# Cross attention with a quantised feed-forward on one core: a reordered prologue, another queue for the second weights, and moved steps in every stage

## What is computed

```python
# attention: 32 query heads of 16, 8 key/value groups, 256 keys from ctx
q = ln(x) @ Wq.T + bq;  k = ctx @ Wk.T + bk;  v = ctx @ Wv.T + bv
scores = einsum("bgrqd,bgkd->bgrqk", q, k) / 4, masked with -inf (two masks)
x = x + softmax(scores) @ v  (heads joined)  @ Wo.T + bo
# feed-forward: both products with quantised rows and weights
bitlinear(x, w, b) = einsum("bsd,od->bso", act_quant(rms_norm(x)), weight_quant(w)) + b
h = gelu(silu(bitlinear(ln(x), w1, b1)))            # 2048 wide
out = x + bitlinear(layer_norm(h) * g + b, w2, b2)
```

## Time and profile before

| | us |
|---|---|
| three runs | 619.96, 621.9, 622.6 (median 621.9) |
| the profiled execution, own time | 622.59 |
| its span, first to last instruction | 620.8 |
| PE busy | 524.9 (85%) |
| DVE busy | 489.0 (79%) |
| ACT busy | 350.8 (57%) |
| POOL busy | 135.0 (22%) |
| mean granted clock of TensorE | 0.926 of full speed |
| the ends of the stages c = 0, 1, 2, 3, 4, 5, 6 on PE | about 109, 182, 248, 310, 373, 435, 498 |

### The profile page before, as it was taken

One profiled execution on the slowest core, in us unless ns is written; L12 is line 12 of the kernel. 1 busy time (PEld: TensorE's weight loads), 2 busy tenths in 40 slices (PEclk: granted clock), 3 DMA queues, 4 the chain that ended last, 5 costly groups with the idle time before them and its releaser, 6 DMA issues.

```text
span 620.8 us, 8914 instructions
## 1 busy us (share of the span) xinstructions
PE 524.9 (85%) x3374; PEld 289.5 (47%) x3374; DVE 489.0 (79%) x728; ACT 350.8 (57%) x424; POOL 135.0 (22%) x101
## 2 busy tenths in 40 slices
PE   4778497689889999999999999999869969698446
PEld 4666133362456355645564556455425523343222
DVE  3769939349699978997899789988896887648784
ACT  0244280517584867486748674867187739287630
POOL 5030031100611061106110611301140113103220
PEclk9989598797989999999999999999969989799688
DMA  8588637934422641365136412642134221100000
GB/s 315 152 234 324 211 84 191 386 116 146 86 67 105 183 99 36 125 195 114 36 124 191 102 54 76 191 98 74 40 86 102 74 75 17 38 0 1 34 34 35
DMA packets 32994, 72.17 MB, mean 116 GB/s; under 512 B 7167, under 2 KB 14529, under 8 KB 29950
## 3 DMA queue, kind: packets, MB, share of 16 engines
q1 hardware_dynamic: 31798, 71.26, 38.8%
q10 hardware_dynamic: 1152, 0.31, 0.2%
HBM read 46.50 MB, written 20.61 MB: 108 GB/s over the span
## 4 chain that ended last, share of the span: by engine, by line
PE 58%; DVE 12%; DMA 10%; ACT 9%; issue 7%; SPq 2%; POOL 1%; ACTq 1%; DVEq 0%
PE FF L853 9%; PE FF L678 7%; PE PV L792 7%; PE FF L901 6%; ACT PT L1069 5%; PE PV L775 5%; PE S L759 5%; PE S L735 5%; DVE negm L1337 4%; PE S L888 3%; PE FF L855 2%; PE PV L735 2%; DMA work<-in_w 2%; PE FF L867 2%; DMA num<-o_raw 2%
## 5 line engine op out<-in xcount | busy, mean ns | idle before, releaser
L1069 ACT ACTIVATE PT<-S 128x1024 f32<-128x1024 f32 x128 | 123.6, 1033 | 28.1 <-PE S L759 28.0
L1337 DVE TENSOR_REDUCE negm<-S 128x4 f32<-128x1024 f32 x88 | 105.6, 1215 | 24.7 <-PE S L735 23.2
L759 PE MATMUL S<-Q,K 100*128 100x512 bf16 x256 | 78.0, 413 | 27.7 <-ACT PT L1069 18.3
L775 PE MATMUL PV<-PT,vaug 128*32 128x256 f32 x1024 | 71.8, 400 | 0.4 <-ACT PT L1069 0.4
L853 PE MATMUL FF<-w1t,xqT 128*128 128x512 bf16 x256 | 67.4, 386 | 2.0 <-ACT PT L1100 1.1
L1100 ACT ACTIVATE work<-FF,s 128x512 f32<-128x512 f32 x56 | 38.5, 687 | 40.6 <-PE FF L855 40.6
L792 PE MATMUL PV<-wo_sb,num 128*128 128x512 f32 x128 | 59.9, 614 | 0.4 <-DVE negm L1337 0.4
L678 PE MATMUL FF<-xnT,wq_sb 128*128 128x256 f32 x224 | 52.8, 394 | 8.6 <-ACT xnT L1039 8.6
L735 PE MATMUL S<-K,Q 97*128 97x256 bf16 x352 | 54.5, 282 | 6.6 <-issue 3.5
L759 PEld LDWEIGHTS S<-Q,K 100*128 100x128 bf16 x256 | 18.7, 101 | 77.4 <-ACT PT L1069 54.8
L1337 DVE TENSOR_REDUCE negm<-PV 128x4 f32<-128x1024 f32 x40 | 48.8, 1221 | 6.3 <-PE PV L735 5.9
(11 more groups left out here) (196 smaller groups left out, 858.5 us busy)
## 6 DMA issues: line engine op xcount, KB each, us to landing
Q<-q_d SPq DMA_DIRECT2D x15, 768.0 KB
work<-in_w SPq DMA_DIRECT2D x8, 1024.0 KB, 11.4
q_d<-part SPq DMA_DIRECT2D x8, 768.0 KB, 3.6
x_sb<-in_x SPq DMA_DIRECT2D x8, 512.0 KB, 4.0
ctx_sb<-in_ctxT SPq DMA_DIRECT2D x8, 512.0 KB, 4.0
q_d<-part SPq DMA_DIRECT2D x8, 512.0 KB, 3.3
xb_sb<-in_x SPq DMA_DIRECT2D x8, 512.0 KB, 3.9
rec<-rec_d SPq DMA_DIRECT2D x30, 128.0 KB, 2.6
```

Of the source, the lines that this page charges most:

```text
L759: last = pe.matmul(where, K[0:ROWS_2, g, kt * P:(kt + 1) * P], Q[0:ROWS_2, g, 2 * pair:2 * pair + 2, :], start=not masked, stop=True)
L775: last = pe.matmul(PV[32 * r:32 * r + 32, g % 4, :], vaug[:, c % 2, kt, g, :], PT[:, n % PT_SLOTS, r, :], start=(kt == 0), stop=(kt == TT ...
L1069: act.activation(PT[:, n % PT_SLOTS, :, :], ST[n % 2][:], ACT.Exp, scale=0.25).then_inc(S["pt_made"], 1)
L1337: dve.tensor_reduce(negm[:, t, R * g:R * g + R], RING_1[n % 3][:], AX.X, ALU.max, negate=True).then_inc(S["max_made"], 1)
```

## The change

In the order of the code:

- Q parts: `q_d` has four blocks of 16 rows instead of six. Part 0 is written once (block 0), part 1 twice (blocks 1 and 3), part 2 once. `query_rows` reads block 0 three times over into Q's rows 0 to 47 in one transfer and the other three blocks in a second one; `ROW_LOADS` is 4.
- Prologue: bk has a semaphore of its own. PE does K, `turn_x(0)`, V, `project_q(0)`; ACT and DVE follow suit (`keys`, `values_in`; `key_rests(0)` ahead of `masks`; `maximum(0, 0)` ahead of `key_rests(1)`). SP issues x(1) before ctx(1), one chunk of w1 behind the key parts, and x(2) and the other three chunks behind `rows_back_first`.
- w2: POOL issues the four chunks at the head of stage c = 0, as soon as `w1_done` is set; its weight sum, scale and quantising move up in stage c = 1. `rows_back(a, 1)` is issued ahead of the last denominators and numerators.
- Stage heads on PE: `project_out(f, 0)`, `turn_max`, the weight sum, `turn_x(w)`, `project_out(f, 1)`, `project_q(w)`, `project_k(a)`; `project_v(a)` stands behind the first pair of `scores_2`, and its copy on ACT behind the second exp.
- ACT: where there is no w, `squares(t, 1)` stands behind the second exp; in stage c = 7 both squares stand between the exps. The means are made by ACT behind each gelu, not by POOL.
- Last stages: `turn_hq` of batch 5 goes to four halves of S1 and S0 (`turned_hq_ps`), so that `layer_1` needn't wait for it; steps on DVE and PE are reordered.

```diff
-Q_TERMS = [slice(0, 3), slice(3, 6, 2), slice(4, 5)]
+Q_BLOCKS = [slice(0, 1), slice(1, 4, 2), slice(2, 3)]
+        def turned_hq_ps(t, n):
+            where = S0w if t == B - 3 and n > 1 else S1w
+            return where[:, 512 * (n % 2):512 * (n % 2) + 512]
...
@@ SP
-            weight_chunk(w1, 0)
-            weight_chunk(w1, 1)
+            def query_rows(a, gs, landed):
+                shared = q_d[a][0:HD, gs, :].rearrange("d g n -> d (g n)")
+                sp.dma_start(Q[0:Q_SHARED * HD, gs, :, :].rearrange("d g r t -> d (g r t)"),
+                             shared.unsqueeze(0).broadcast_to([Q_SHARED] + list(shared.shape))).then_inc(landed, 16)
+                sp.dma_start(Q[Q_SHARED * HD:ROWS_SPLIT, gs, :, :].rearrange("d g r t -> d (g r t)"),
+                             q_d[a][HD:4 * HD, gs, :].rearrange("d g n -> d (g n)")).then_inc(landed, 16)
...
                 if at_start(a):
+                    load_x(1)
                     load_context(1)
-                    load_x(1)
                     key_parts(0)
-                    load_x(2)
+                    weight_chunk(w1, 0)
                     query_parts(0)
                     negatives()
                     rows_back_first()
-                    weight_chunk(w1, 2)
-                    weight_chunk(w1, 3)
+                    load_x(2)
+                    for n in range(1, 4):
+                        weight_chunk(w1, n)
...
                     denominators(c, 2)
-                    denominators(c, 3)
-                    numerators(c, 1)
                 if a is not None:
                     rows_back(a, 1)
                 if c is not None:
+                    denominators(c, 3)
+                    numerators(c, 1)
...
@@ POOL
+            def second_weights():
+                pool.wait_ge(S["w1_done"], 1)
+                for n in range(4):
+                    cols = slice(2048 * n, 2048 * n + 2048)
+                    pool.dma_start(work[:, cols], w2[:, cols]).then_inc(S[f"w2_chunk{n}"], 16)
...
+                if at_start(c):
+                    second_weights()
                 if w is not None and w + 1 < B:
                     norm_1(w + 1)
...
-                    mean_3(f, 0)
                     norm_3_last(f, 0)
-                    mean_3(f, 1)
                     norm_3_last(f, 1)
...
@@ PE
                 w = next_front(a) if c != 0 else None
-                if w is not None:
-                    turn_x(w)
                 if f is not None:
                     project_out(f, 0, c)
                 if c is not None:
                     turn_max(c)
+                if at_start(c) or at_start(f):
+                    weight_sum(c)
+                if w is not None:
+                    turn_x(w)
+                if f is not None:
+                    project_out(f, 1, c)
                 if w is not None:
                     project_q(w)
-                if f is not None:
-                    project_out(f, 1, c)
                 if a is not None and a > 1:
-                    project_kv(a)
-                if at_start(c) or at_start(f):
-                    weight_sum(c, a)
+                    project_k(a)
                 for g in range(G + 1):
...
+                    if g == 0 and a is not None and a > 1:
+                        project_v(a)
...
                     for n in range(4):
-                        turn_hq(t, n, f)
+                        turn_hq_last(t, n)
                     for n in range(4):
-                        layer_1(f, n, t)
+                        layer_1(f, n, None)
...
-                    layer_1(f, 0, None)
-                    layer_1(f, 1, None)
+                    for n in range(8):
+                        layer_1(f, n, None)
                     layer_2_last(t - 1, 1)
-                    for n in range(2, 8):
-                        layer_1(f, n, None)
...
@@ ACT
+                act.wait_ge(S["gelu_made"], 2 * f + t + 1)
+                act.activation(st[:, 1, t:t + 1], st[:, 0, t:t + 1], ACT.Identity, scale=-1.0 / INNER
+                               ).then_inc(S["mu_made"], 1)
...
-                    squares(t, 0)
                     act.activation(table_call[:, 1:2], table_call[:, 0:1], ACT.Exp)
                     for n in range(16):
                         exps(c, n)
-                        if n == 3:
-                            squares(t, 1)
+                        if n in (1, 3):
+                            squares(t, n // 2)
...
-                if t is not None and a is not None:
+                if t is not None and w is not None:
                     squares(t, 1)
...
-                    keys_and_values(a)
+                    keys(a)
                 if c is not None:
                     for n in range(16):
                         exps(c, n)
+                        if n == 1 and w is None and t is not None:
+                            squares(t, 1)
+                        if n == 1 and a is not None and a > 1:
+                            values_in(a)
...
@@ DVE, last_scores
                 maximum_2(t, 0)
                 power_2(t)
+                maximum_2(t, 1)
                 turn_1(f)
-                maximum_2(t, 1)
+                reciprocal_last(c)
                 factor_2(t)
                 scale_2(t)
-                reciprocal_last(c)
...
@@ DVE, last_hidden and last_values
+                maximum_2(t, 0)
                 residual_2(t - 1, 1)
-                maximum_2(t, 0)
...
                 gain(t, 0)
+                shift(t, 0)
                 spread_last(t, 1)
-                shift(t, 0)
                 gain(t, 1)
...
@@ DVE, body
                 if c is not None:
                     max_rows(c)
+                if at_start(c) or at_start(f):
+                    weight_scale(c)
...
+                if at_start(f):
+                    quantise_weight(1, w2t[:].rearrange("p k n -> p (k n)"))
                 if w is not None:
                     query_rests(w)
```

More of the change, by code:

```diff
@@ L36 @@
 PT_SLOTS = 4
-ROW_LOADS = 3
+ROW_LOADS = 4
 PIECES = 4
@@ L393, in weights_and_biases, with layer_rows @@
                     sp.dma_start(b1_rows[n:n + 1, :], b1_d[cb:cb + 1, :]).then_inc(S["k_b1r"], 16)
-            def second_weights():
-                sp.wait_ge(S["w1_done"], 1)
-                for n in range(4):
-                    weight_chunk(w2, n)
+            def layer_rows():
                 for to, of in ((b2_bc, b2), (g_bc, ln_g), (b_bc, ln_b)):
@@ L453, in body @@
                 if c is not None:
+                    denominators(c, 3)
+                    numerators(c, 1)
+                if c is not None:
                     reciprocals(c)
                 if at_start(c):
-                    second_weights()
+                    layer_rows()
                 if t is not None:
@@ L698, in project_kv, with project_v @@
                 for k in range(KD):
-                    pe.matmul(to[:, 0:T], wkv_sb[:, k, 0:P], ctx_sb[:, k, :],
-                              start=(k == 0), stop=(k == KD - 1))
+                    last = pe.matmul(to[:, 0:T], wkv_sb[:, k, 0:P], ctx_sb[:, k, :],
+                                     start=(k == 0), stop=(k == KD - 1))
+                last.then_inc(S["k_ps"], 1)
+            def project_v(a):
+                if a == 1:
+                    pe.wait_ge(S["v_placed"], 1)
+                to = pair_of(a)
                 for t in range(TT):
@@ L751, in scores_2 @@
                     pe.wait_ge(S["m_in"], 16 * c + 16)
+                if n == 1 and c == 1:
+                    pe.wait_ge(S["w_mean"], 4)
                 if n >= 2:
@@ L875, in turn_hq_last @@
                 pe.wait_ge(S["hs_made"], 2 * t + tok + 1)
-                pe.wait_ge(S["hqT_made"], 4 * t + n - 1)
+                if t > B - 3:
+                    pe.wait_ge(S["hqT_made"], 4 * t + n - 1)
                 for k in range(8):
-                    last = pe.transpose(S1w[:, 512 * half:512 * half + 512].bitcast(BF16)[:, k * P:(k + 1) * P],
+                    last = pe.transpose(turned_hq_ps(t, n).bitcast(BF16)[:, k * P:(k + 1) * P],
                                         source[:, tok, (8 * half + k) * P:(8 * half + k + 1) * P], identb[:])
@@ L1048, in queries, with keys, values_in @@
                                    ).then_inc(S["q_made"], 1)
-            def keys_and_values(a):
-                act.wait_ge(S["kv_ps"], a + 1)
+            def keys(a):
+                act.wait_ge(S["k_ps"], a + 1)
                 wait_for(act, S["k_out"], 48 * a)
                 if at_start(a):
-                    act.wait_ge(S["w_bias"], 48)
+                    act.wait_ge(S["w_bk"], 16)
                 act.activation(part[:, 0, R, :], pair_of(a)[:, 0:T], ACT.Identity, bias=bk_sb[:, 0:1]
                                ).then_inc(S["k_made"], 1)
+            def values_in(a):
+                act.wait_ge(S["kv_ps"], a + 1)
                 if at_start(a):
@@ L1169, in body @@
                 if at_start(a):
```

(33 more changed lines are left out.)

69 lines of the change are left out of this document (28 added, 41 removed).

## The result

The changed kernel takes 680.05 us (median of 4 runs, 677.7 to 689.2), the kernel before 621.0 in the same comparison: ratio 1.094, 95% interval 1.088 to 1.100. One run of it (689.2 us) and one of the kernel before with the broadcast load (668.3 us) were in a slower state, and all ratios, and the costs in us that are called means, leave these two out. The profiled execution has a span of 676.2 us and a mean granted clock of 0.893 (0.926 before). The forecast was 606.5 us, with 615 as the upper end.

The account below looks back on a forecast made before the run. TensorE was taken to bound the middle stages, with idle time at the edges. From 622.6 us, terms summing to -15.7 and the median's -0.7 gave 606.2, say 606.5 us; range 599 to 615.

Parts of the forecast that it names:

- The step that failed: Row loads of later stages: one broadcast load of three equal Q blocks carries the same bytes, one issue more; no cost.
- Start, +4.3: Prologue to scores_2 of batch 0: row loads leave 4.6 us earlier, but x(2) lands at about 42; loss 4.3 us.
- c = 0, 0 with 3 either way: Stage c = 0: w2 data in by about 95, last denominators perhaps 1 us late; 0, with 3 us either way.
- c = 1, -12.8: Stage c = 1: scores_2 at 129.2, 11.0 us earlier, and another 1.8 won in the loop; bounds 9.5 and 14.5.
- c = 2, +1.6: Head of stage c = 2: project_out waits for maximum 14 and exps(0) comes later; +1.6 us, bounds 0 and +3.
- c = 3 to 5, -0.37 each: Heads of stages c = 3 to 5: PE's 2.6 us isn't won, ACT's queue sets exps(0); -0.37 us each, -1.1 for three.
- c = 6, -2.5: Stage c = 6: squares go behind exps(1), so exps come 3.1 us earlier; DVE's last scale caps the gain at 2.3 to 2.7.
- c = 7 and tail, -3.1 and -2.1: Stage c = 7: turn_hq through four banks, project_out earlier, -3.1 us. Tail: deviations(7,1) and shift(7,0) wait less, -2.1 us.
- (1): Start and c = 1: x(2) lands early and c = 1 gives its bound; about 602 us, chance 0.2.
- (3): Middle stage heads win their full 2.6 us because ACT's wait is shorter than counted; -6.7, 599.5 us, chance 0.07.
- Rival (2): Start loses 6.8 us and den 3 stalls DVE, or DVE caps c = 1; about 612 us, chance 0.22.
- rival (4): Stage c = 1: w2 on POOL's queue comes late and delays scores_2; at 130 the time is 626 us; chance 0.03.

Follow-up runs that it names:

- six blocks: The changed kernel with the Q parts as before: six blocks of 16 rows in DRAM, one load of 96 rows; 624.8 us, ratio 1.004.
- The last order: Against the 613.1 us kernel (reordered, w2 in halves), project_q(w) put ahead of project_out(f, 1) in the stage heads; 605.6 us, ratio 0.977.

## Why the prediction was wrong

- **The step that failed:** "the broadcast load of the three equal Q blocks carries the same bytes with one issue more". I costed it by bytes and issues, and so at nothing. It cost some 52 us in the changed kernel and 40 in the kernel before. It stood in no rival, so the range couldn't hold it. No row of the kernel before shows such a load; a bound should have been worked out from the shape: if a source in three blocks might use three of the 16 engines, it takes up to five times as long as its bytes say.
- **Without that load the forecast is missed too:** with six blocks all the reordering comes out at 624.8 us, ratio 1.004, where 606.5 and a gain were forecast and 615 was the upper end. That miss is in the start and in c = 0.
- **Start, +4.3:** mechanism right, size wrong. x(2) landed at 44.0, not 42, the first maximum came at 49.2, not 47.4, and the copy 7.9 later, not 5.9 (the 1.6 for the store of the maxima falls into c = 0 in this cut).
- **c = 0, 0 with 3 either way:** wrong by 10 to 12 us even with six blocks. I had "the last denominators, behind it, may come 1 us too late"; with w2 in flight 8 KB took 13.1 us and the wait was 9.7. The four loads of w2 took 24.5 us from issue to the last landing (87.61 to 112.08), not the 16 that 400 GB/s gave. I asked when each transfer's bytes could be through at the engines' rate, not how much was queued when the small one came. Gated, in halves and with the layer vectors behind it, 7.7 of the 10.2 are won back.
- **c = 1, -12.8:** right, -12.1 with six blocks. Even under the slow load -5.3.
- **c = 2, +1.6; c = 3 to 5, -0.37 each:** measured with six blocks +1.5, -0.3, +1.3, +0.5. The first two are right, and in c = 3 for the reason given: ACT goes from squares and table load to the keys (273.40) and exps without idle time. But a wait was missing from the sum: K behind DVE's rests, 1.93 us in each head. I had written that the rests end 1.1 later and looked only at `turn_xq` for who waits. In c = 3 ACT's path covered the wait; in c = 4 K and the scores ran 1.7 us longer after it, at the lower clock, and ACT waited for PE. In c = 5 K and the scores weren't slow, and its +0.5 stays open. The last order shows that 1.2 us below the kernel before could be had in c = 3 and 4.
- **c = 6, -2.5:** right, -2.8.
- **c = 7 and tail, -3.1 and -2.1:** right together, -4.9 against -5.2; singly they weren't tested.
- **The rivals:** in (1) x(2) was to be early, and in (3) the middle heads were to win 2.6 each; neither came. Rival (2) had the right kind of wait, the last denominators stalling DVE, at 3 us where six blocks show 9.7, and a start that loses more; but both kernels lie far above its 612 us. In rival (4) the load of w2 through POOL was to come late. With six blocks it came 1 to 4 us late for ACT's sums, and the harm was done on the other side, to the transfers beside it. The estimate of 12.4 us for its four issues, worked out from the Trainium skill (SBUF — State Buffer, SBUF: two separate sides), is for issues that overlap a two-port operation of DVE. Here the four took 2.40 us, with hardly more than the statistics of a norm on DVE beside them (87.21 to 88.98), so no run tests it.
- With the three sizes put right (start +2.0, c = 0 +11.8, middle stages +2.4) the sum for six blocks is 606.2 + 16.2 = 622.4; 624.8 was measured. That only says that the terms left alone were right together; the three sizes are read from the same run.

## What to carry to other kernels

Before a load is costed by its bytes, look at its outermost size: three of something, repeated or merely spaced, ran on three engines here, and small transfers issued later waited behind it. The same bytes as 16 x 3, or as three loads, cost nothing more. For each small transfer on the critical chain, add up what is in flight when it is issued. Where an order on one engine is changed, list every wait of the next instruction, not only those of the one that moved.

## What the runs showed of the hardware

- Loads of 3 x 16 rows of 8 KB left the DMA share at 0.19, with some 25 GB/s for each of three engines, 9 to 12 us after the issue; the same bytes as 16 x 3 ran at a share of 0.8 to 1.1 and were mostly through after 6 us. A repeated read in itself cost nothing measurable (ratio 1.002, 0.999 to 1.005).
- With 4 MB from POOL's queue in flight, and 960 KB ahead of it in its own, a transfer of 8 KB from SP's queue took 13.1 us. With the 4 MB held back DVE's wait for it fell from 9.7 (1.3 with x(2) early) to 0.27 us. The Trainium skill says why (DMA: Bandwidth & Descriptors, Rules for kernel authors): loads of all issuers run on the same 16 engines and interleave. The 13.1 us are this case's price for it.
- While POOL multiplied 128x1024 twice (2.34 us each, until 113.91 and 116.23), DVE operations of 128x64 that take 0.20 and 0.23 us in other stages took 2.07 and 2.31, and each ended within 0.1 us of POOL's. In the earlier trace rows the 128x2 multiply of 2.34 us is of the same kind.
